# Reordering the opening of a fused attention and expert kernel: context load, key weight product, row turning, x turning and the first Silu table

## What is computed

```python
nx = layer_norm(x, ln_gamma, ln_beta)
q, k, v = nx @ Wq, context @ Wk, context @ Wv
scores = einsum('bth,bph->btp', q, k) * H ** -0.5
evidence = softmax(scores) @ v
combined = concat([nx, evidence, broadcast(cond)])            # 768 wide
router_probs = softmax(combined @ router_W + router_b)         # 3 experts
h = silu(combined @ e_w1 + e_b1)                               # per expert, 512 wide
routed = sum((h @ e_w2 + e_b2) * router_probs)
g = sigmoid(silu(combined @ gate_w1 + gate_b1) @ gate_w2 + gate_b2)
out = x + g * (routed @ out_w + out_b)
```

## Time and profile before

| What | Value |
| --- | --- |
| Median of 3 runs | 441.52 us (441.14 to 441.97) |
| The profiled execution, its own time | 441.1 us |
| Its span (first to last instruction) | 439.3 us |
| PE busy | 431.0 us, 98% |
| PEld, DVE, ACT, POOL busy | 347.2, 316.0, 243.7, 104.6 us |
| Share of the chain that ended last that is PE | 96% |

### The profile page before, as it was taken

How to read it: one execution, slowest core, us unless ns; L and a number is a source line. 1 busy time by engine, 2 the same in 40 slices (tenths; PEclk the granted TensorE clock), 3 DMA queues, 4 the chain that set the end, 5 groups by cost and what they waited for, 6 DMA issues and landing times.

```text
span 439.3 us, 5709 instructions
## 1 busy us (share of the span) xinstructions
PE 431.0 (98%) x1912; PEld 347.2 (79%) x1912; DVE 316.0 (72%) x584; ACT 243.7 (55%) x377; POOL 104.6 (24%) x95
## 2 busy tenths in 40 slices
PE   7999999999999999999999999999999999999995
PEld 7478878888888878888888878887888878888884
DVE  3588659899897867784687867784687757664366
ACT  2346844868474656465474557464565557455341
POOL 2300303050334032312024032312024022402430
PEclk9999999999999999999999999999999999999999
DMA  8569889207537425633545425633542525123202
GB/s 266 143 154 273 189 189 205 48 34 192 139 71 191 102 69 121 171 70 96 107 90 139 119 61 111 174 73 91 114 100 74 126 64 112 37 64 97 57 0 48
DMA packets 77138, 50.31 MB, mean 115 GB/s; under 512 B 55950, under 2 KB 65718, under 8 KB 77110
## 3 DMA queue, kind: packets, MB, share of 16 engines
q1 hardware_dynamic: 74960, 47.56, 45.0%
q0 software_dynamic: 800, 1.58, 1.5%
q10 hardware_dynamic: 1350, 0.82, 0.6%
HBM read 27.29 MB, written 7.93 MB: 80 GB/s over the span
## 4 chain that ended last, share of the span: by engine, by line
PE 96%; DVE 1%; DMA 1%; ACT 1%; issue 0%; DVEq 0%
PE bank L597 38%; PE bank L833 35%; PE bank L813 12%; PE bank L664 2%; PE bank L617 2%; PE bank L706 2%; PE bank L642 1%; PE bank L676 1%; DMA work<-in_L_xcond_Wk_dram 1%; PE bank L621 1%; PE bank L714 0%; PE bank L741 0%; DVE work L1353 0%; DVE quad L1355 0%; PE bank L629 0%
## 5 line engine op out<-in xcount | busy, mean ns | idle before, releaser
L597 PE MATMUL bank<-nx,w1n 128*128 128x512 f32 x672 | 173.4, 394 | 0.0
L1030 ACT ACTIVATE hf<-bank,zb 128x512 f32<-128x512 f32 x112 | 77.1, 688 | 136.6 <-PE bank L813 132.5
L597 PEld LDWEIGHTS bank<-nx,w1n 128*128 128x128 f32 x672 | 125.9, 188 | 27.9 <-issue 0.5
L833 PE MATMUL bank<-h,w 128*128 128x512 f32 (+1 forms) x579 | 146.1, 388 | 0.0
L833 PEld LDWEIGHTS bank<-h,w 128*128 128x128 f32 x579 | 107.7, 188 | 24.3
L1383 DVE TENSOR_TENSOR h<-hf,h 128x512 fp32r<-128x512 f32 x111 | 87.2, 789 | 49.1 <-ACT h L1033 45.3
L1033 ACT ACTIVATE h<-bank,zb 128x512 fp32r<-128x512 f32 x111 | 75.7, 682 | 0.0
L813 PE MATMUL bank<-wT,vw 128*128 128x512 f32 x224 | 70.9, 398 | 0.0
L813 PEld LDWEIGHTS bank<-wT,vw 128*128 128x128 f32 x224 | 41.9, 188 | 9.8 <-issue 0.5
L1416 POOL TENSOR_TENSOR xq<-xq,quad 128x512 f32<-128x512 f32 x14 | 18.6, 1349 | 108.0 <-DVE quad L1102 108.0
L1431 POOL TENSOR_TENSOR work<-work 128x512 f32<-128x512 f32 x14 | 18.9, 1348 | 72.7 <-DVE work L1302 60.0
(11 more groups left out here) (150 smaller groups left out, 439.6 us busy)
## 6 DMA issues: line engine op xcount, KB each, us to landing
vw<-vw_pair SPq DMA_DIRECT2D x48, 256.0 KB, 3.7
xn<-in_x_dram SPq DMA_DIRECT2D x8, 512.0 KB, 5.2
p_bc<-prob_dram SPq DMA_DIRECT2D x8, 512.0 KB, 4.7
xq<-in_x_dram SPq DMA_DIRECT2D x32, 128.0 KB, 2.8
out_dram<-xq SPq DMA_DIRECT2D x28, 128.0 KB, 2.8
stage<-in_L_xcond_e_w_dram SPq DMA_DIRECT2D x24, 128.0 KB, 4.7
xhat_dram<-xn SPq DMA_DIRECT2D x6, 512.0 KB, 2.9
quad<-xhat_dram SPq DMA_DIRECT2D x24, 128.0 KB, 2.7
```

The lines of the kernel that those rows point to most:

```text
L597: mm = pe.matmul(dst, lhs(a), rhs(c), start=first and i == 0, stop=last and i == n - 1)
L833: mm = pe.matmul(o[:, tokens], lhs, h_tile(s, a)[:, tokens], start=c == 0 and i == 0, stop=c == COUNT[g] - 1 and i == 2)
L1030: act.activation(hf[:, s % 2, :], z, ACT.Silu, bias=zb[:, j, b:b + 1]).then_inc(s_h, 1)
```

## The change

ScalarE's queue issues two of the row loads (gate_b1, e_b1) ahead of the context, the two router loads right behind it, and the other five rows after that. wqT is copied by VectorE and pT0 by ScalarE. The product gT goes to two banks (4 and 6), each half copied as soon as it is done. The rows are turned ahead of `keys(0)`; x is turned right behind `keys(1)`; the matmuls on zeros go from 12, 3, 3 to 11, 2, 0. VectorE handles `nx_full(0)` ahead of `keys_lo`. ScalarE evaluates a Silu of eight ones ahead of `pair_hi(0, 2)`.

```diff
+        silu_of_one = sb("silu_of_one", [8, 1])
...
+        GT_BANK = (4, 6)
...
         PREP = {n: i + 1 for i, n in enumerate(
-            ("wkT", "wqT", "pT0", "pT1", "gT", "qk0", "cols", "qk1", "vT0", "vT1", "lb", "lb_bc"))}
-
-        PV = {n: i + 1 for i, n in enumerate(("wkT", "pT0", "cols", "qk0", "qk1", "lb", "lb_bc"))}
-        PA = {n: i + 1 for i, n in enumerate(("wqT", "pT1", "gT", "qk0", "qk1", "vT0", "vT1"))}
+            ("wkT", "wqT", "pT0", "pT1", "gT0", "gT1", "cols", "qk0", "qk1", "vT0", "vT1", "lb", "lb_bc"))}
+
+        PV = {n: i + 1 for i, n in enumerate(("wkT", "wqT", "cols", "qk0", "qk1", "lb", "lb_bc"))}
+        PA = {n: i + 1 for i, n in enumerate(("pT0", "pT1", "gT0", "gT1", "qk0", "qk1", "vT0", "vT1"))}
...
             pe.wait_ge(s_warm, 1)
-            keep_busy(12)
+            keep_busy(11)
             pe.wait_ge(s_pool0, 2)
             pe.wait_ge(s_wk, 16)
             turn("wkT", 0, (s_pv, PV["wkT"]), wk_raw)
             pe.wait_ge(s_wq, 16)
-            turn("wqT", 1, (s_pa, PA["wqT"]), wq_raw)
-            keep_busy(3)
+            turn("wqT", 1, (s_pv, PV["wqT"]), wq_raw)
+            keep_busy(2)
             pe.wait_ge(s_ctx, 16)
             for k in range(KC):
-                dst = take(2 + k, (s_pv, PV["pT0"]) if k == 0 else (s_pa, PA["pT1"]))
+                dst = take(2 + k, (s_pa, PA[f"pT{k}"]))
                 for t in range(4):
                     mm = pe.transpose(dst[:, t:4 * PART:4], ctx_raw[:, t, k * PART:(k + 1) * PART], ident[:, :])
                 prep(f"pT{k}", mm)
-            pe.wait_ge(s_pv, PV["wkT"])
-            pe.wait_ge(s_pa, PA["wqT"])
-            dst = take(4, (s_pa, PA["gT"]))
+            pe.wait_ge(s_pv, PV["wqT"])
             for j in range(KC):
+                dst = take(GT_BANK[j], (s_pa, PA[f"gT{j}"]))
                 for k in range(KC):
-                    mm = pe.matmul(dst[:, j * H:(j + 1) * H], wkT[:, k, j * PART:(j + 1) * PART], wqT[:, k, :],
+                    mm = pe.matmul(dst[:, 0:H], wkT[:, k, j * PART:(j + 1) * PART], wqT[:, k, :],
                                    start=k == 0, stop=k == KC - 1)
-            prep("gT", mm)
-            keep_busy(3)
+                prep(f"gT{j}", mm)
 
             def keys(i):
-                product(f"qk{i}", i, (s_pv, PV[f"qk{i}"]),
-                        lambda j: gT[:, j, i * PART:(i + 1) * PART], lambda j: pT[:, j, :])
+                dst = take(i, (s_pv, PV[f"qk{i}"]))
+                for j in range(KC):
+                    pe.wait_ge(s_pa, PA[f"gT{j}"])
+                    mm = pe.matmul(dst[:, :], gT[:, j, i * PART:(i + 1) * PART], pT[:, j, :], start=j == 0, stop=j == KC - 1)
+                prep(f"qk{i}", mm)
...
-            pe.wait_ge(s_pa, PA["gT"])
-            pe.wait_ge(s_pv, PV["pT0"])
-            pe.wait_ge(s_pa, PA["pT1"])
-            keys(0)
             pe.wait_ge(s_rows, 16 * ROW_LOADS)
             pe.wait_ge(s_eb2, 16 * KC)
...
             prep("cols", mm)
+            keys(0)
             keys(1)
+            x_transpose(0)
             pe.wait_ge(s_wv, 16)
             values(0)
-            x_transpose(0)
             values(1)
...
         def _(act):
 
+            early = ("gate_b1", "e_b1")
+            for name in early:
+                load_rows(act, name)
             act.dma_start(ctx_raw, ctx.rearrange("b q h -> (b q) h").rearrange("(p t) h -> p t h", p=PART))\
                .then_inc(s_ctx, 16)
+            load_router(act)
             for name in small:
-                load_rows(act, name)
+                if name not in early:
+                    load_rows(act, name)
...
-            prep("wqT", wqT.rearrange("p k n -> p (k n)"), 1)
-            load_router(act)
+            prep("pT0", pT[:, 0, :], 2)
             prep("pT1", pT[:, 1, :], 3)
-            act.wait_ge(s_prep, PREP["gT"])
             for j in range(KC):
-                ins = act.copy(gT[:, j, :].rearrange("p (k q a) -> p k q a", k=KC, a=QROWS),
-                               quad_cols(bank[4][:, j * H:(j + 1) * H]))
-            ins.then_inc(s_pa, 1)
+                act.wait_ge(s_prep, PREP[f"gT{j}"])
+                act.copy(gT[:, j, :].rearrange("p (k q a) -> p k q a", k=KC, a=QROWS),
+                         quad_cols(bank[GT_BANK[j]][:, 0:H])).then_inc(s_pa, 1)
...
             vr_copy(0)
+            act.activation(silu_of_one[:, :], ones8[:, 0:1], ACT.Silu)
             pair_hi(0, 2)
...
             prep_copy("wkT", wkT.rearrange("p k n -> p (k n)"), 0)
-            prep_copy("pT0", pT[:, 0, :], 2)
+            prep_copy("wqT", wqT.rearrange("p k n -> p (k n)"), 1)
             stats_of(0)
...
             normalise(0)
+            dve.wait_ge(s_pv, PV["cols"])
+            nx_full(0)
             keys_lo(0)
             keys_lo(1)
-            dve.wait_ge(s_pv, PV["cols"])
-            nx_full(0)
             nx_lo(0)
```

## The result

The changed kernel takes 443.5 us (median of 5 runs, 442.56 to 444.94) against 441.52 before (440.64 to 441.97 in 5 runs). The ratio is 1.0044, 95% interval 1.0023 to 1.0065: slower by 2 us where 2.2 us less were forecast. A later repetition gave 442.92 over 12 runs (439.81 to 445.54), ratio 1.0023 [0.9999, 1.0047]; the kernel before stayed within 440.64 and 442.69 in the 23 runs beside it. So the change made the time longer by 1 to 2 us, of which the repetition alone is at the edge of what can be told from no change, and more scattered.

What follows compares the result with a forecast made beforehand. The prediction took TensorE's own work to set the pace once the slots run, so only their start counted. Gains of 2.0 + 0.25 = 2.25 us took the median of 441.52 to 439.3 us, range 438.3 to 440.6.

Steps and rivals of the forecast that it cites:

- Step 1: Opening loads: context behind two row loads; Wk lands at 3.9 us, context at 6.2, gT begins 7.9 to 8.7, not 9.04.
- Step 2: Rows ahead of the keys: their landing sets the turning, at 10.15 us; gT's copy is off the path.
- Step 3: x turned right behind the keys: last scores wait for nx_lo, lb begins at 20.25 us, 2.0 us gained by then.
- step 4: From lb to the first second-layer matmul: the path is TensorE's, stages move along, no filler left in it.
- Step 5: Early Silu on ScalarE: table load fits its 1.83 us of idle time; worth 0.0 to 0.5 us, taken as 0.25.
- A: Rival, smaller gain: moved transfers land later than said, or the clock rises late; 439.8 to 440.6 us, chance 0.19.
- C: Rival, slower: a pause before the rows lets the clock fall back, half pace loses 2.95 us; 442.2 us, chance 0.04.
- the first mark: Start of the product lb, first work behind the scores: 22.25 us before, forecast at 20.25, a gain of 2.0 us.

Runs made afterwards that it cites:

- e4_no_early_silu: The changed kernel without the early Silu of eight ones: 442.81 us (12 runs).
- e5_ctx_on_sync: The changed kernel with the context's load moved to SyncE's queue between Wq and x: 440.67 us (12 runs).
- e3_fill_wait: The changed kernel with 12 matmuls on zeros in place of 2 ahead of the wait for the context: 440.61 us (12 runs).
- g2_changed_again: The changed kernel itself once more, with a new trace: 442.92 us (12 runs, 439.81 to 445.54).
- f9_ctx_late_alone: The changed kernel with the context first on ScalarE's queue again, but held until 1.61 us: 443.91 us, ratio 1.0037.
- e2: The kernel before, with the two row loads put ahead of the context and nothing else: 444.64 us, ratio 1.005.
- f11_first_fill: The changed kernel with the context issued first again and 17 matmuls on zeros for 11 ahead of Wk: 438.86 us (6 runs).
- e8_first_x_late: The changed kernel with the context first, x turned between the values and nx_full(0) behind keys_lo as before: 441.18 us.
- f10_first_fill_keys: The changed kernel with the context first, 17 matmuls on zeros for 11 ahead of Wk, and keys(0) ahead of the rows' turning: 438.42 us, ratio 0.993.
- f12_before_fill: The kernel before with 17 matmuls on zeros for 12 ahead of Wk: 440.92 us, ratio 0.9993.
- e6_x_waits_ctx: The changed kernel with SyncE's load of x and all behind it held until the context has landed: 439.9 us (12 runs).
- g1_wk_late: The changed kernel with the context first and SyncE's queue (Wk, Wq, x and on) held until 1.6 us: 441.25 us (12 runs).

## Why the prediction was wrong

**Step 1 failed, in two terms.** The step said that the context is issued some 0.9 us later "and so lands at 0.75 + 0.9 + 4.6 = 6.2, ahead of its use". The delay of the issue was right (1.67 us). The 4.6 us were not a constant: they belonged to a context that ran beside Wk. Beside x the same load took 6.5 us, and 5.0 to 8.6 in the traces of the kernels that issue it as late on that queue. Without x and the loads behind x beside it, it took 4.7. This term was mis-sized by 2.0 us, of which the sum feels 1.2: it had TensorE begin on the context at 7.0, and it began at 8.25.

The second term is the clock. The step let gT begin "between 7.9 and 8.7" with the rise at about the old time. It rose only after gT: all eight transposes and all eight matmuls ran at the lower level. Eight transposes cost 0.9 more than at the upper level (1.76 for 0.88) and gT 1.7 more (3.41 for 1.74). Sum by marks: with the late context at the upper level the rows would be turned at 8.25 + 0.9 + 1.74 = 10.9, 0.75 later than the 10.15 of the sum; the other 2.7 to 13.57 are the clock's. So the late landing alone would have left `lb` at about 10.9 + 10.0 = 20.9, a gain of 1.3; it is the clock that turns the gain into a loss. The traces of the variants with a late context show it (us):

| Trace | TensorE begins on the context | Rows turned | Between | Level of the transposes and gT |
| --- | --- | --- | --- | --- |
| e4_no_early_silu | 6.75 | 9.51 | 2.76 | upper |
| e5_ctx_on_sync | 7.97 | 10.72 | 2.75 | upper |
| e3_fill_wait | 9.79 | 12.54 | 2.75 | upper |
| g2_changed_again | 8.49 | 12.93 | 4.44 | upper in the transposes, lower in gT |
| the changed kernel | 8.25 | 13.57 | 5.32 | lower |
| f9_ctx_late_alone | 9.94 | 15.26 | 5.32 | lower |

The same work takes 2.75 us at one level and 5.32 at the other, wherever it begins. How the clock came to be low differs. In the changed kernel's first trace it had not yet risen when the wait began (first rise at 13.8), in f9 and e2 it fell in the wait, in g2 just after it, and in e3, e4 and e5 it stayed up through waits of 2.75, 1.2 and 1.9 us. The changed kernel, g2 and e4 are one program up to there; that their clocks differ is chance as far as these traces tell.

**Step 2 held in what is off the path, not in its time.** gT's copy is off the path. The rows' landing was hidden in the changed kernel, behind gT. Where it can be seen it is earlier than the 10.15 of the step: the rows are turned at 9.5 in e4_no_early_silu, with the same load order, and at 9.75 in f11_first_fill, where TensorE waits for out_b's row. This term was 0.4 to 0.65 too long.

**Step 3 held in size, not in its last knot.** 10.0 us from the rows to `lb` for 10.1; undoing x's early turning costs 0.4 by the marks and 0.5 in the time (e8_first_x_late). But the step had the last scores wait for VectorE's `nx_lo`, and they don't: the chain from the rows to `lb` is TensorE's alone, values to 22.27 and then 0.93 + 0.46 of scores. VectorE does `keys_lo` and `nx_lo` in 1.28 and 1.29 us, where the step had 1.47 and 1.41, and the path is the one for which the step had 20.0, TensorE's without waits. That the two lie so close is luck. In step 4 one small thing was missed: a wait of 0.3 us in the slots.

**Step 5 held within its bounds.** 0.26 by the marks in the changed kernel, forecast 0.25, but 0.04 to 0.27 over the eleven traces that have it, so that the hit is in part luck. The table load sat in the idle time as forecast, with 0.20 for the Silu, and the 1.28 were worth a fifth of themselves or less, because TensorE had other work. The drain that the Trainium skill ("ScalarE: Activation LUTs", section "What ACT_TABLE_LOAD costs") adds does not show: the small Silu starts 33.39 - 32.10 = 1.29 us behind the load's start.

**The rivals.** The cause named in A was the right one, and it named both halves, the late context and the late clock. Its price was too small because it let the two cover each other and bounded the clock at 11.5, where it rose at 13.8. Added up as here they exceed the gain. C had the sign and the bound "beyond 12.9 us", which was met. Its mechanism, a pause in which the level falls back, is seen in e2 and f9, but not in the changed kernel's first trace, where the level had not been reached; and I put the pause at the wait for the rows and gave it 0.04. A and C were one story, and I gave its far end almost nothing. The sentence of the Trainium skill that speaks against transposes ("TensorE: Matmul & The Clock Gate", section "Part 4: PE-mode transpose") would have led to a late rise too, but for another reason. In f10_first_fill_keys the eight transposes take 0.87 us in all, the upper level's pace, so they do run at it; what brought the level there can't be told, because 17 matmuls on zeros stood ahead.

## What to carry to other kernels

Don't carry a load's time to landing over to a new place in the order: it depends on what runs beside it, and here a load issued 0.9 us later landed 3 us later. Count a wait of TensorE twice where the clock is not settled, once for the wait and once for the work behind it at half pace. Matmuls on zeros in the opening's pauses gave 1.5 us in f11 where nothing else bound, and 0.4 by the marks in f12, where a load did. When several edits arrive as one change, undo the one on which the first wait depends: one load put back turned this loss of 1 to 2 us into a gain of 1, and six more matmuls on zeros ahead of Wk made it 2.6. And look at the sum even where the time fits: the trace nearest the forecast had the rows, the first mark and the tail elsewhere.

## What was not expected of the hardware

- Issued at 0.75 us beside Wk, the context took 4.5 to 4.8 us to land in all such traces; issued at 1.65 with x beside it, 5.0, 6.5, 6.8, 8.1, 8.3 and 8.6 us. One 4 KB packet took 0.16 us in the first case and 0.24 to 0.52 on average in the slowest stretches of the second, 0.17 to 0.26 over the whole load. It needs neither the small loads ahead (f9_ctx_late_alone) nor a second queue (e5_ctx_on_sync); it nearly goes with x and the loads behind it held back (e6_x_waits_ctx), and did not delay anything by as much when the weights were the late ones (g1_wk_late). What holds single packets up, and why some of the 16 shares fall so far behind, stays open.
- With the context out of the way Wk landed 2.7 us after its issue instead of 4.4: 1.7 us less, where step 1 worked out 1.2 from the bytes.
- The granted clock fell while TensorE waited (f9_ctx_late_alone, at 8.6 us) or 0.9 us after it had work again (g2_changed_again, at 9.4), and stayed on its lower level through 5.5 us and 3.4 us in which TensorE was never out of work. It fell twice in the slots as well, for 3.4 us each, behind waits of no more than 0.8 us (f11_first_fill, f12_before_fill).
